# State-space layer of a two-layer kernel: decay rows broadcast by DMA, mask on GpSimd, exponential into PSUM, scans in pairs

## The reference

```
proj = x @ in_proj_w.T                    # gate 8192, x 8192, B and C 8x128 each, dt 128
x, B, C = silu(conv4(...));  dt = clip(softplus(dt + dt_bias), 1e-3, 100)
cs   = cumsum(dt * A)                     # A = -(1..128), one value a head
y[l] = sum_{s<=l} exp(cs[l]-cs[s]) * (C[l].B[s]) * dt[s]*x[s]  +  D*x[l]
yg   = y * silu(gate);  yg = yg * rsqrt(mean(yg^2 over a group) + 1e-5) * norm_w
out  = yg @ out_proj_w.T
```

## Time and profile before

| | us |
|---|---|
| median of 3 runs (2480.08 to 2488.39) | 2484.99 |
| the profiled execution | 2485.11 |
| its span, first to last instruction | 2483.3 |
| busy: PE / DVE / ACT / POOL | 2285.2 / 1697.0 / 1379.5 / 846.0 |
| mean granted TensorE clock, share of full speed | 0.954 |
| DMA, mean over the span | 34 GB/s |

### The profile page before, as it was taken

The page is one execution under the profiler, slowest core; times in us unless marked ns, Lnnn a source line. Parts: engine busy times, 40 slices in busy tenths (PEclk is TensorE's granted clock), DMA queues, the critical chain, the costliest instruction groups (busy, mean ns, idle before and its releaser), DMA issues. The chain is left out here.

```text
span 2483.3 us, 38330 instructions
## 1 busy us (share of the span) xinstructions
PE 2285.2 (92%) x11624; PEld 1633.1 (66%) x11624; DVE 1697.0 (68%) x2949; ACT 1379.5 (56%) x3105; POOL 846.0 (34%) x681
## 2 busy tenths in 40 slices
PE   6898888897899999999999999999999999987998
PEld 4554545445677776777767777677776777756877
DVE  3555555554797598489579759848957975965345
ACT  4453535403785487388468558737846855852330
POOL 4251423310244244244325414414432541441230
PEclk9699998899999999999999999999999999988999
DMA  5000000001210110111011011011101101002100
GB/s 226 10 1 9 1 1 1 1 0 47 72 34 20 52 31 28 44 31 35 11 60 35 20 52 31 28 48 31 31 24 48 35 20 52 27 1 85 42 18 34
DMA packets 38226, 85.39 MB, mean 34 GB/s; under 512 B 3584, under 2 KB 5888, under 8 KB 37376
## 3 DMA queue, kind: packets, MB, share of 16 engines
q1 hardware_dynamic: 38016, 82.82, 10.1%
HBM read 79.92 MB, written 2.88 MB: 33 GB/s over the span
## 5 line engine op out<-in xcount | busy, mean ns | idle before, releaser
L1643 PE MATMUL b_ps<-xh_keep,wh 128*128 128x512 f32 x1152 | 490.9, 426 | 5.2 <-DVE bc L1398 3.0
L1645 PE MATMUL b_ps<-xh_keep,wl 128*128 128x512 f32 x1152 | 463.1, 402 | 0.0
L1644 PE MATMUL b_ps<-xl_keep,wh 128*128 128x512 f32 x1152 | 463.0, 402 | 0.0
L1434 DVE TENSOR_TENSOR decayed<-decay,b_scores 128x768 f32<-128x768 f32 x256 | 397.8, 1554 | 25.1 <-ACT decay L1162 24.1
L1323 POOL TENSOR_TENSOR wl<-wraw,wh 128x512 fp32r<-128x512 f32 x144 | 190.9, 1326 | 574.7 <-ACT wh L1111 574.7
L1156 ACT ACTIVATE decay<-b_ps,cs 128x256 f32<-128x256 f32 (+1 forms) x1024 | 345.1, 424 | 7.7 <-PE b_ps L1653 7.1
L1398 DVE SCALAR_TENSOR_TENSOR xs<-b_ps,par,xs 128x510 f32<-128x510 f32 (+2 forms) x384 | 284.9, 742 | 93.2 <-ACT xs L1130 80.9
L1643 PEld LDWEIGHTS b_ps<-xh_keep,wh 128*128 128x128 f32 x1152 | 222.0, 193 | 84.2 <-issue 41.5
L1645 PEld LDWEIGHTS b_ps<-xh_keep,wl 128*128 128x128 f32 x1152 | 221.5, 192 | 53.4
L1644 PEld LDWEIGHTS b_ps<-xl_keep,wh 128*128 128x128 f32 x1152 | 223.1, 194 | 42.2
L1524 DVE SCALAR_TENSOR_TENSOR yl<-yg,par,yh 128x512 fp32r<-128x512 f32 x128 | 96.4, 758 | 203.5 <-ACT yh L1177 202.4
(11 more groups left out here) (229 smaller groups left out, 4116.3 us busy)
## 6 DMA issues: line engine op xcount, KB each, us to landing
wraw<-win_dram SPq DMA_DIRECT2D x144, 256.0 KB, 2.6
oraw<-wout_dram SPq DMA_DIRECT2D x8, 2048.0 KB, 9.4
w<-w_dram SPq DMA_DIRECT2D x2, 3584.0 KB, 23.9
fraw<-wgu_dram SPq DMA_DIRECT2D x11, 512.0 KB, 3.5
draw<-wd_dram SPq DMA_DIRECT2D x1, 2816.0 KB, 11.9
xT<-xT_dram SPq DMA_DIRECT2D x4, 512.0 KB, 3.8
x_keep<-x_dram SPq DMA_DIRECT2D x1, 2048.0 KB, 11.2
out_dram<-x_keep SPq DMA_DIRECT2D x8, 256.0 KB, 2.0
```

The source lines that it names most:

```text
L1434: nc.vector.tensor_tensor(sd[:, b % 2, :, :], ex[:, b % 2, :, :], sm[:, b, :].unsqueeze(1).to_broadcast([P, 2, 3 * P]), ALU.mult)\
L1643: nc.tensor.matmul(out, w_h, x_h, start=(k == 0), stop=False)
L1644: nc.tensor.matmul(out, w_h, x_l, start=False, stop=False)
L1645: last = nc.tensor.matmul(out, w_l, x_h, start=False, stop=(k == KT - 1))
```

## The change

The rows of cumulated sums are written once to DRAM in float32 (`sum_rows`) and read back by DMA with every partition reading the same row: for each unit and sequence two DMAs (256 and 128 columns of both heads) to `rows`, four buffers. GpSimd adds a mask of 0 and -1e30 (`later`) to the two diagonal blocks (`mask_rows`). ScalarE takes the exponential with the per-partition sum as bias (`exps`), two instructions a head, from `rows` into PSUM (E{j}_{b}_{h}, banks 4 and 5). VectorE multiplies out of PSUM, one head at a time (`decays`, L1464 in the new numbering). TensorE's broadcast matmuls, the clamps and the bf16 parts are gone. The scans of sequences 2 and 3 of unit j-1 now run in unit j, after T{j}; all scans come in pairs; Y{j}_0 and Y{j}_1 share bank 7. `decayed` has four buffers, tanh results four. The squares are summed over channels by 8 one-column matmuls (`ms`), put behind the first four output tiles. SP's list is unrolled.

```diff
+            out = [("CB2", 6), ("CB3", 7)]
+            for j in range(UNITS):
+                out += [(f"T{j}_0", 6), (f"T{j}_1", 3), (f"Y{j}_0", 7), (f"Y{j}_1", 7)]
+                out += [(f"E{j}_{b}_{h}", 4 + h) for b in range(BATCH) for h in range(2)]
+                out += in_jobs(j + 1) if j < LAST else ([] if last else in_jobs(-1) + in_jobs(0))
...
@@ SP: load_rows(n, b), n = group * 8 + unit
+                    sp.wait_ge(*bk.filled(ph, f"E{j}_{b}_1"))
+                for at, shift, cols in ((0, 0, SEQ), (SEQ, P, P)):
+                    sp.dma_start(rows[:, b, :, at:at + cols],
+                                 bass.AP(tensor=ssm["rows"].tensor, offset=(2 * n * BATCH + b) * SEQ + shift,
+                                         ap=[[0, P], [BATCH * SEQ, 2], [1, cols]])).then_inc(rows_loaded[b], 16)
...
@@ ScalarE
-                for src, dst, bias in blocks(ph, g, j, b):
-                    last = nc.scalar.activation(dst, src, ACT.Relu, bias=bias)
-                nc.scalar.activation(ex[:, b % 2, :, :], ex[:, b % 2, :, :], ACT.Exp, scale=-1.0).then_inc(*exp_done.inc())
+                for h in range(2):
+                    name = f"E{j}_{b}_{h}"
+                    if not h:
+                        waited(rows_masked.made(g, j * BATCH + b))
+                    waited(bk.freed(ph, name))
+                    nc.scalar.activation(e[:, 0:SEQ], rows[:, b, h, 0:SEQ], ACT.Exp, bias=c0)
+                    nc.scalar.activation(e[:, SEQ:ROW], rows[:, b, h, SEQ:ROW], ACT.Exp, bias=c1).then_inc(*bk.full(ph, name))
+                    yield
...
@@ GpSimd: mask_rows, and its steps of unit j
+                at = rows[:, b].rearrange("p h (k c) -> p h k c", c=P)[:, :, 0:3:2, :]
+                nc.gpsimd.tensor_tensor(at, at, later[:].unsqueeze(1).unsqueeze(1).to_broadcast([P, 2, 2, P]), ALU.add)\
...
+                    if j:
+                        gate(ph, j - 1, 0)
+                    mask_rows(g, j, 3)
+                        weights_lo(g, 6 + 2 * j)
+                        mask_rows(g, j + 1, 0)
+                        add_square(ph, j - 1, 0)
+                        gate(ph, j - 1, 1)
+                        mask_rows(g, j + 1, 1)
+                        weights_lo(g, 7 + 2 * j)
+                        add_square(ph, j - 1, 1)
+                        mask_rows(g, j + 1, 2)
...
@@ VectorE: steps of unit j (before = decays(j-1, 3), now[b] = decays(j, b), one head a next)
+                        next(before)
+                        skip(ph, g, j - 1, 0)
+                        silu(ph, conv_halves(j)[3])
+                        next(before)
+                        taps(ph, gn, h[0], (1, 2))
+                    next(now[0])
+                        taps(ph, gn, h[0], (3,))
+                    next(now[0])
+                    times_dt(ph, g, j, 0)
+                        silu(ph, h[0])
+                    next(now[1])
+                    times_dt(ph, g, j, 1)
+                        skip(ph, g, j - 1, 1)
+                    next(now[1])
+                        taps(ph, gn, h[1], (1, 2))
+                    next(now[2])
+                        taps(ph, gn, h[1], (3,))
+                        silu(ph, h[2])
+                        silu(ph, h[1])
+                    next(now[2])
...
@@ TensorE: steps of unit j
+                    for k, name in enumerate(names[0:2]):
+                        in_half(ph, g, 4 + 2 * j, name)
+                    turn(ph, j)
+                    if j:
+                        scan(ph, j - 1, 2)
+                        scan(ph, j - 1, 3)
+                    for name in names[2:4]:
+                        in_half(ph, g, 5 + 2 * j, name)
+                    scan(ph, j, 0)
+                    scan(ph, j, 1)
```

More of the change, by code:

```diff
@@ L1000, in halves @@
[L1000 to L1001 removed]
+            out = [("CB2", 6), ("CB3", 7)]
[3 more added lines that the diff above has]
+                out += in_jobs(j + 1) if j < LAST else ([] if last else in_jobs(-1) + in_jobs(0))
+            return out + [("ms", 0)] + [(f"o{t}", t) for t in range(NT)]
@@ L1254, in steps @@
-                    more = 6 + 2 * j < SUBS or not last
+                    final = j == LAST
+                    h = None if final and last else conv_halves(j + 1 if not final else -1)
+                    gn = g + 1 if final else g
+                    more = 6 + 2 * j < SUBS or not last
+                    before, now = exps(ph, g, j - 1, 3), [exps(ph, g, j, b) for b in range(3)]
+                    if j:
+                        next(before)
+                        tanh(ph, conv_halves(j)[3])
+                        next(before)
@@ L1274, in steps @@
+                    next(now[1])
+                    if h:
+                        tap(ph, gn, h[1], f"Y{j - 1}_1" if j and not final else None)
+                    next(now[1])
                     if more:
                         weights_hi(g, 7 + 2 * j)
-                    if j < UNITS - 1:
-                        exps(ph, g, j + 1, 0)
-                    tanh(ph, h[3])
-            def project(ph, g, first):
-                for j in range(first, UNITS):
+                    next(now[2])
@@ L1487, in steps @@
-                    gn = g if not final else g + 1
-                    if j:
-                        decay(ph, j, 0)
-                    conv_tap(ph, gn, h[0], 1)
-                    if not j:
-                        decay(ph, j, 0)
-                    decay(ph, j, 1)
+                    final = j == LAST
+                    h = None if final and last else conv_halves(j + 1 if not final else -1)
+                    gn = g + 1 if final else g
+                    before, now = decays(ph, j - 1, 3), [decays(ph, j, b) for b in range(3)]
@@ L1646, in in_half @@
                 last.then_inc(*bk.full(ph, name))
-            def rows(ph, j, b):
-                name = f"R{j}_{b}"
-                pe.wait_ge(*bk.freed(ph, name))
-                for h in range(2):
-                    last = nc.tensor.matmul(ps[bk.bank(ph, name)][:, h * SEQ:(h + 1) * SEQ], sel[:, 2 * j + h:2 * j + h + 1].to_broadcast([32 * SPLITS, P]),
-                                            comb[:, b * SEQ:(b + 1) * SEQ], start=True, stop=True)
-                last.then_inc(*bk.full(ph, name))
@@ L1738, in project @@
                         pe.wait_ge(*y_lo.made(ph, (j, h)))
-                        for t in range(h * NT // 2, (h + 1) * NT // 2):
+                        if not j and not h:
+                            pe.wait_ge(*sq_added.made(ph, (LAST, 1)))
+                            pe.wait_ge(*bk.freed(ph, "ms"))
+                            for t in range(NT):
+                                last = nc.tensor.matmul(ps[bk.bank(ph, "ms")][:, t:t + 1], ssq[:, t * P:(t + 1) * P],
+                                                        cst("ones")[:, 0:1], start=True, stop=True)
+                            last.then_inc(*bk.full(ph, "ms"))
+                        tiles = [t for t in (O_TILES if j else O_FIRST) if t // (NT // 2) == h]
+                        for t in tiles:
                             if j == 0:
```

850 lines of the change are left out of this document (409 added, 441 removed).

## The result

The changed kernel takes 2473.03 us (median; 2462.49 to 2477.85), the kernel before, run beside it, 2487.35 (2480.08 to 2488.39). The ratio is 0.9947, 95% interval 0.993 to 0.9964. It is faster by 13 to 14 us, where 103 were forecast; the time lies outside the predicted range. The profiled execution is the shortest of the six, 2462.49 us, with a span of 2460.7, so sums over its profile come out some 10 us better than the median.

The account below looks back on a forecast made before the run. TensorE was taken to bound the kernel, VectorE close behind. From 2485 us, 157 came off (82 broadcasts + 35 scans - 8 squares + 45 edges + 3 prologue) and 54 were added for VectorE's waits: 2382, range 2325 to 2450.

Parts of the forecast that it names:

- the one on the DMAs: Row loads on SP, per unit: a pair lands in some 3.5 us, hidden by some 7 us.
- GpSimd's list waits for row DMAs: Rival, GpSimd's units: masks wait for rows, 18.5 us a unit, slower from 17.5 on; 2547 us, chance 0.15.
- VectorE-ScalarE chain: Units 1 to 6: VectorE and ScalarE wait for each other, unit 16.6 us against TensorE's 15.1; costs 54 us.
- Collisions: VectorE's silus of x beside GpSimd's masks: 0 to 2.2 us a unit, taken as 0.5.
- TensorE: TensorE's work in all groups: broadcasts save 82 us, paired scans 35, one-column matmuls for squares cost 8.
- A pair of scans: Sign in the profile after, on TensorE: pairs of scans take 1.3 to 1.45 us.
- Edges: Idle time at group edges: 5.5 of 7.8 us go in seven groups, 7 in the last; 45 us saved.
- The start and the last group: Layer's ends: prologue saves 3 us (0 to 8), the last group's edge 7 us.
- TensorE stays the bound: Rival, whole layer: VectorE's waits fit beside TensorE's unit of 15.1 us; 2328 us, chance 0.15.
- GpSimd blocks the silus: Rival, VectorE's unit: silus of x wait for GpSimd, unit as long as before; 2416 us, chance 0.2.

Follow-up runs that it names:

- sp_rows_first: Changed kernel with only SyncE's list altered: row loads go out ahead of the weight loads; 2499.99 us, ratio 1.0063.
- masks_later: Changed kernel with only GpSimd's list altered: each addition of the mask stands half a unit later; 2399.27 us, ratio 0.9648.
- gate_ahead: Changed kernel with one pair swapped on GpSimd's list: gate of half 0 ahead of the mask of sequence 2; 2388.21 us, ratio 0.9618.
- exp_first: Changed kernel with only ScalarE's list altered: second exponential of sequence 1 ahead of the tap of the next unit's second x half; 2440.24 us, ratio 0.9813.
- no_masks: Changed kernel without GpSimd's 256 mask additions, row loads kept, exponentials with constant bias and tiny scale; 2368.16 us, ratio 0.9535.

## Why the prediction was wrong

**The step that failed** is the one on the DMAs: a pair of row loads "should take some 3.5 and has most of a unit [...] Hidden by some 7 us". The landing was off by 1.4 us (4.9 from an exponential's end to the mask; 3.7 and 4.4 from issue, the second issued behind the first). The cover was wrong. I measured it from the load to the exponential that needs the row, a unit later. But the first to wait for the row is the mask, and in the loop shown (of sp_rows_first) GpSimd stood idle ahead of it for 4.62 of the 4.88 us since the exponential: the cover was 0.3 us, not 7, and a gate stood behind. In the changed kernel's five late units above, masks waited 24.3 us, up to 3.8 us each. masks_later moved the mask to where the row has long landed and gained 74 us; gate_ahead only put the gate ahead of one mask and gained 85.

**The rival that named it was built too simply.** "GpSimd's list waits for row DMAs" named the mechanism, and its threshold of 17.5 us a unit was met (17.5 measured, a gain of 13 us where its formula gives 2, since it counts all 64 units and only five of eight are slow). Its masks were put at 2.0 us each and took 1.31; its 4 us of waits a unit were 4.9 (24.3 in five). What was missing is that the delay closes on itself through ScalarE's squares. The unit isn't GpSimd's work plus waits (5 + 8 + 1.5 + 4) but the length of a circle over five engines. GpSimd was busy only 12 to 13.7 us.

**The other steps, tested by removing the failed one** (masks_later, 2399 against 2382):
- VectorE-ScalarE chain: unit 16.6 forecast, 16.65 measured; idle 1.6 against 1.69. Taking it away gave 2399.3 - 2356.7 = 43 us, where 54 was put: in masks_later it lengthens four units of a group (to 16.1, then 16.65, from 15.36), not six.
- Collisions: 0.5 us a unit forecast, 0.65 measured for the masks.
- TensorE: 13.6 us less work a group forecast ((82 + 35 - 8) / 8), 13.8 measured (199.0 to 185.2). Some 3 of these are the clock, an estimate: the lower level held for 10.2 us in the group before and for 3.4 in this one, and 3.4 us of it made a unit's work 1.5 us longer above. At full clock a unit went from 16.93 to 15.36 us, 0.26 above the 15.1 forecast. A pair of scans takes 1.45 us (1651.24 to 1652.69), the upper end of the 1.3 to 1.45 that I named.
- Edges: 45 us was too much. 5.5 of 7.8 idle us a group were to go; 4.5 are left (189.70 - 185.17), so 3.3 went. That is 2.2 x 7 = 15 us too much, but the chain, put too dear, makes up for most of it. From the first group's T0 to the last one's (before, then masks_later) 83 us are gained, where the forecast has 87:

```profile
628.75:2075.13 1446.38, 1391.87 (x7224) 1038.14 (x7225) 1111.87 (x1416) 947.29 (x1918) 546.45 (x393) 0.98 0.12 36
639.74:2003.16 1363.42, 1298.87 (x6832) 1007.12 (x6833) 1010.89 (x1625) 790.24 (x1696) 808.33 (x616) 0.99 0.37 101
```

- The start and the last group: what parts 2399 from 2382 lies mostly here. From the layer's first matmul to the first T0, and from the last T0 to the next layer, it took 45.4 + 202.2 = 247.6 us before and 52.3 + 192.7 = 245.0 in masks_later (24 matmuls of the projection changed sides): 2.6 us gained, where the forecast has 103 - 87 = 16. In the last group, which has no successor's projection to work on, TensorE now waits some 17 us for VectorE (`xdt`, skip, silus), where its waits were 15 us before, 6.8 of them for the squares; no run isolates this.
- "TensorE stays the bound", 2328, needed one more edit, and gave 2357.
- "GpSimd blocks the silus": they do grow in the changed kernel (mean 942 ns, 748 before), but the median is 693 ns, not over 1 us, the sign named for this rival.

## What to carry to other kernels

For every transfer or result that an in-order engine waits for, measure the cover at the place of the first instruction that waits, then read what stands behind it on that engine and who waits for that; if the chain comes back to what started the transfer, its length is the least time of one turn, however idle the engines are. If two chains meet at one instruction, both have to be cut. A long wait in a profile need not be a cost: one swap of neighbours left 293 of 357 us of waiting and won 85 us. When a loop is cut, look for the next one close below it, and let two edits be tried together, since exp_first alone gave 33 us and on top of masks_later 43.

## What the runs showed that I had not expected

- TensorE's clock was at its lower level in ten of 35 late units of the changed kernel and in none of masks_later. Between the first and the last T0 it is busy for 1322.0 us in the one and 1298.9 in the other, with the same work.
- The engines settle into a loop that is 18.4 us long although none of them is busy for more than 15.6 in a unit at full clock (17.1 where the clock falls), and a change that took 400 us off one wait of SyncE (465.6 to 57.4) gave them back at another (527.0 to 916.3) and made the kernel 27 us slower.
- 256 KB and 128 KB of rows, read as two pieces of 1 KB or of half a KB for each of 128 partitions, land 3.7 and 4.4 us after issue, with or without the masks (3.8 and 4.5 in no_masks).
